# The expert layer moved from the second attention to the first, on one PSUM bank

## What is computed

```
x  = L0_attn_x;  xn = layernorm(x)
# layer 0
a  = attention_0(xn)                    # 16 heads of 64, softmax over queries, W_O
y  = xn + attn(conv(layernorm(xn)))     # 16 heads of 8, causal, rotary, depthwise convolution
h  = layernorm(y)
e  = argmax(h @ router_w)               # one of 4 experts for each position
m  = silu(h @ Wg[e]) * (h @ Wv[e]) @ Wd[e]     # 128 -> 2 x 512 -> 128
x  = x + a + y + m
# layer 1
xn = layernorm(x)
x  = x + flash(xn)                      # 16 heads of 8, causal, two passes over blocks of 64
       + fp4_ffn(xn)                    # 128 -> 352 -> 128, inputs and weights rounded to blocks of FP4
```

## Time and profile before

| | us |
|---|---|
| runs: median (lowest to highest) | 3603.09 (3598.25 to 3603.4) |
| the profiled execution | 3598.52 |
| its span, first to last instruction | 3596.7 |
| TensorE busy (share of the span) | 3086.5 (86%) |
| VectorE busy | 2093.3 (58%) |
| ScalarE busy | 1787.1 (50%) |
| GpSimd busy | 860.3 (24%) |
| mean granted TensorE clock | 0.937 |

### The profile page before, as it was taken

One profiled execution on the slowest core, in us unless ns is written; L12 is line 12 of the kernel. 1 busy time (PEld: TensorE's weight loads), 2 busy tenths in 40 slices (PEclk: granted clock), 3 DMA queues, 4 the chain that ended last, 5 costly groups with the idle time before them and its releaser, 6 DMA issues.

```text
span 3596.7 us, 53224 instructions
## 1 busy us (share of the span) xinstructions
PE 3086.5 (86%) x19535; PEld 1705.8 (47%) x19535; DVE 2093.3 (58%) x4810; ACT 1787.1 (50%) x4252; POOL 860.3 (24%) x1140
## 2 busy tenths in 40 slices
PE   2689898998989899998989889898988989898864
PEld 1245455454545545454545545454554545454432
DVE  5454665756566575657656565665656566554432
ACT  0245555555545455555545555554555555455421
POOL 0000222313222131323123132312213131222323
PEclk7699999999999999999999999999999999999965
DMA  4130303020020302002030301103020110200000
GB/s 104 20 44 1 52 2 47 9 36 20 13 43 2 55 2 44 12 17 40 1 55 2 44 12 22 35 2 55 2 44 12 24 31 7 47 2 14 6 11 3
DMA packets 112901, 89.39 MB, mean 25 GB/s; under 512 B 11203, under 2 KB 107269, under 8 KB 112645
## 3 DMA queue, kind: packets, MB, share of 16 engines
q1 hardware_dynamic: 93956, 70.25, 12.8%
q0 software_dynamic: 4096, 8.40, 0.8%
q10 hardware_dynamic: 14592, 7.34, 0.7%
HBM read 27.05 MB, written 16.19 MB: 12 GB/s over the span
## 4 chain that ended last, share of the span: by engine, by line
PE 59%; DVE 12%; POOL 10%; issue 9%; ACT 5%; DMA 2%; SPq 1%; POOLq 0%; ACTq 0%; DVEq 0%
PE ps L1584 6%; PE ps L1601 6%; PE ps L1819 4%; PE ps L1743 4%; PE ps L1722 4%; PE ps L1656 3%; PE ps L1645 3%; PE ps L1623 3%; DVE nma L1210 3%; PE ps L1632 3%; PE ps L1574 2%; PE ps L1703 2%; PE ps L1884 2%; PE ps L1561 2%; PE ps L1587 2%
## 5 line engine op out<-in xcount | busy, mean ns | idle before, releaser
L877 ACT ACTIVATE share_a<-ps,nma 128x128 f32<-128x128 f32 (+3 forms) x1024 | 530.9, 525 | 443.7 <-DVE nma L1210 442.5
L1210 DVE TENSOR_REDUCE nma<-ps 128x2 f32<-128x256 f32 (+3 forms) x512 | 420.1, 823 | 407.5 <-PE ps L1587 405.4
L945 ACT ACTIVATE share_z<-ps 128x512 f32<-128x512 f32 (+1 forms) x704 | 378.3, 559 | 372.1 <-PE ps L1724 241.7
L1275 DVE TENSOR_REDUCE nmx<-ps 128x1 f32<-128x384 f32 (+3 forms) x704 | 426.1, 635 | 173.9 <-PE ps L1705 162.4
L722 POOL TENSOR_TENSOR vn<-va,rla 128x512 f32<-128x512 f32 x128 | 133.4, 1042 | 1359.1 <-DVE rla L1181 1359.1
L1601 PE MATMUL ps<-share_a,vn 128*64 128x512 f32 (+3 forms) x2048 | 351.4, 492 | 35.7 <-POOL vn L722 34.7
L1703 PE MATMUL ps<-kst,qst 96*128 96x128 bf16 (+3 forms) x1024 | 269.6, 317 | 71.1 <-DMA kst<-part 34.4
L1722 PE MATMUL ps<-qst,kst 99*128 99x512 bf16 (+3 forms) x1024 | 261.6, 304 | 28.2 <-ACT share_z L945 14.9
L798 POOL TENSOR_TENSOR share_s<-share_s 128x352 f32<-128x352 f32 (+1 forms) x80 | 80.1, 1001 | 770.7 <-DVE share_s L1084 770.5
L1601 PEld LDWEIGHTS ps<-share_a,vn 128*64 128x64 f32 x2048 | 150.8, 151 | 227.9 <-issue 154.2
L1584 PE MATMUL ps<-kq_odd 64*128 64x128 f32 (+3 forms) x1024 | 220.5, 508 | 38.7 <-ACT share_a L877 36.9
(11 more groups left out here) (250 smaller groups left out, 5727.0 us busy)
## 6 DMA issues: line engine op xcount, KB each, us to landing
qst<-part SPq DMA_DIRECT2D x144, 128.0 KB
kst<-part SPq DMA_DIRECT2D x144, 128.0 KB
share_r<-h_sorted SPq DMA_DIRECT2D x16, 448.0 KB, 3.5
y_sorted<-share_a ACTq DMA_DIRECT2D x16, 448.0 KB, 3.0
xin<-in_L_attn_x SPq DMA_DIRECT2D x16, 256.0 KB, 3.9
xk<-xn SPq DMA_DIRECT2D x16, 256.0 KB, 17.5
xres<-in_L_attn_x SPq DMA_DIRECT2D x16, 256.0 KB
out<-xn SPq DMA_DIRECT2D x16, 256.0 KB, 17.4
```

Of the source, the lines that this page charges most:

```text
L877: activation(pa[:, h % 4, OFF[t]:OFF[t] + P * (t + 1)], ps[:, b + k, 0:P * (t + 1)], ACT.Exp, bias=nma[:, h, t:t + 1], accum_out=la[:, h, ...
L945: activation(pt[:, n % 2, h % 4:h % 4 + k, 0:wd], src, ACT.Exp, scale=SCALE_B)\
L1210: v.tensor_reduce(nma[:, 2 * p:2 * p + 2, t], ps[:, b:b + 2, 0:P * (t + 1)], AX.X, ALU.max, negate=True).then_inc(amax, 1)
L1275: v.tensor_reduce(nmx[:, h:h + k, t], src, AX.X, ALU.max, negate=True).then_inc(bmax_ready, 1)
```

## The change

The expert layer goes into the first half of the round. Its seven tiles run one after another on bank 5 (`MOE_BANK`): each step waits for the evacuation of the step before it. Bank 6 alone is `row_max`'s (and `project_v`'s and `shift_rows`'s), and bank 7 takes the after stream (`divide`, `join`, `project_y`, `transpose3`, `route`, `rank`) beside layer 1's; `exps` keeps banks 5 and 6. `sort` is in two parts. The expert buffers leave `share_a` and `share_g`, which the first attention uses, and lie in `share_r` and `hpad`, which the second attention and the convolution use in the other half. So the next round's `kq 0` and first `scores` no longer wait for the experts, while the first `exps` and the first `attend` evacuation do. All four orders are written anew. On TensorE `project_v` comes first, `row_max 0` comes earlier, `sort 0` stands behind `scores1 4`, the tiles are spread from there to `z 7`, and `ao` now stands ahead of `exps 0`. On VectorE `round_x` comes before `shift_rows`, `split 1` before the last tiles of layer 1. On GpSimd `scatter` moves from behind `spread_queries1` to between `norm 0` and `norm 1`, `gather` to behind `round_x 3`.

```diff
-GATE_BANK, VALUE_BANK = (2, 3), (0, 1)
+MOE_BANK = 5
...
     pe=[
...
+        ("project_v",), ("kq", 0), ("v", 0), ("divide", 0), ("kq", 1), ("scores", 0, 0), ("divide", 1), ("v",
+        1), ("divide", 2), ("scores", 0, 1), ("divide", 3), ("scores", 0, 2), ("join",), ("scores", 0, 3),
+        ("project_y",), ("kq", 2), ("scores", 1, 0), ("scores", 1, 1), ("scores", 1, 2), ("z", 0),
+        ("transpose3",), ("route",), ("v", 2), ("scores", 1, 3), ("rank",), ("kq", 3), ("scores", 2, 0),
+        ("scores", 2, 1), ("scores", 2, 2), ("z", 1), ("v", 3), ("row_max", 0), ("row_max", 1),
+        ("transpose2",), ("keys1",), ("scores", 2, 3), ("row_max", 2), ("queries1",), ("values1",),
...
+        ("row_max", 10), ("scores1", 3), ("scores1", 4), ("sort", 0), ("scores", 3, 1), ("sort", 1),
+        ("row_max", 11), ("scores1", 5), ("row_max", 12), ("gate", 0), ("scores1", 6), ("row_max", 13),
+        ("value", 0), ("scores1", 7), ("turn", 0), ("down", 0), ("row_max", 14), ("gate", 1), ("scores", 3,
+        2), ("z", 2), ("row_max", 15), ("value", 1), ("row_max", 16), ("v", 4), ("turn", 1), ("row_max", 17),
...
+        3), ("row_max", 41), ("probs_T1", 1, 3), ("value", 6), ("row_max", 42), ("mix1", 1), ("row_max", 43),
+        ("z", 7), ("shift_rows",), ("turn", 6), ("project1",), ("down", 6), ("ao",), ("exps", 0), ("exps", 1),
+        ("transpose_xq",), ("exps", 2), ("exps", 3), ("transpose1",), ("gate1", 0), ("exps", 4), ("attend", 0,
...
     pool=[
-        ("norm", 0), ("norm", 1), ("spread_queries1",), ("scatter",), ("norm", 2), ("shift1", 0), ("shift1",
+        ("norm", 0), ("scatter",), ("norm", 1), ("spread_queries1",), ("norm", 2), ("shift1", 0), ("shift1",
...
-        5), ("norm", 6), ("norm", 7), ("round_x", 3), ("round_h", 0, 3), ("round_h", 1, 3), ("round_h", 2, 3),
-        ("gather",), ("round_h", 3, 3),
+        5), ("norm", 6), ("norm", 7), ("round_x", 3), ("gather",), ("round_h", 0, 3), ("round_h", 1, 3),
+        ("round_h", 2, 3), ("round_h", 3, 3),
...
+        hsT = view(share_r, [C, SORTED * P])
+        ysort = view(share_r, [P, SORTED, C])
+        ymT = view(share_r, [P, 2, CHUNKS, P], 1024)
...
+        sg = (view(share_r, [P, DFF], 2048), hpad[:, 2:T + 2])
+        ym = sg
...
@@ TensorE @@
                 def gate(j):
-                    if j == 1:
-                        pe.wait_ge(ao_added, count(i, DENSE["ao_added"], 1))
-                    elif j:
-                        pe.wait_ge(yT_ready, count(i, DENSE["yT_ready"], j - 1))
...
+                    if j:
+                        pe.wait_ge(y_ready, count(i, DENSE["y_ready"], j))
...
                 def value(j):
...
+                    pe.wait_ge(gate_read, count(i, DENSE["gate_read"], j + 1))
...
                 def row_max(u):
-                    wd, b = P * (t + 1), 5 + u % 2
+                    wd, b = P * (t + 1), 6
...
-                    if u >= 2:
-                        pe.wait_ge(bmax_ready, count(nxt, AHEAD["bmax_ready"], u - 1))
+                    else:
+                        pe.wait_ge(bmax_ready, count(nxt, AHEAD["bmax_ready"], u))
...
                 def exps(u):
                     if u == 0:
                         pe.wait_ge(shift_loaded, count(nxt, AHEAD["shift_loaded"], 48))
+                        if i is not None:
+                            pe.wait_ge(y_ready, count(i, DENSE["y_ready"], SORTED))
...
                 def divide(t):
                     if t == 0:
                         pe.wait_ge(by_ready, count(i, AHEAD["by_ready"], 4))
-                    if t >= 2:
-                        pe.wait_ge(yn_ready, count(i, AHEAD["yn_ready"], t - 1))
+                        if prv is not None and (type(prv[0]) is not int or prv[0] + prv[1]):
+                            pe.wait_ge(out_ready, count(prv, BEHIND["out_ready"], 0))
+                    else:
+                        pe.wait_ge(yn_ready, count(i, AHEAD["yn_ready"], t))
...
@@ first places of the ring, TensorE @@
                     elif prv is not None:
-                        pe.wait_ge(y_ready, count(prv, DENSE["y_ready"], SORTED))
+                        pe.wait_ge(aexp_done, count(prv, DENSE["aexp_done"], 4 * HEADS))
+                        if n:
+                            pe.wait_ge(ao_added, count(prv, DENSE["ao_added"], 1))
```

More of the change, by code:

```diff
@@ L148 @@
[L148 to L152, removed]
@@ L163 @@
[L163 to L167, removed]
@@ L168 @@
[L168 to L172, removed]
@@ new lines @@
+        0), ("row_max", 20), ("value", 2), ("scores", 4, 1), ("row_max", 21), ("scores", 4, 2), ("turn", 2),
+        ("row_max", 22), ("z", 3), ("row_max", 23), ("down", 2), ("v", 5), ("gate", 3), ("scores", 4, 3),
+        ("kq", 6), ("row_max", 24), ("value", 3), ("probs_T1", 0, 0), ("row_max", 25), ("scores", 5, 0),
+        ("turn", 3), ("row_max", 26), ("probs_T1", 0, 1), ("row_max", 27), ("scores", 5, 1), ("row_max", 28),
+        ("down", 3), ("scores", 5, 2), ("row_max", 29), ("probs_T1", 0, 2), ("gate", 4), ("z", 4), ("row_max",
@@ new lines @@
+        30), ("probs_T1", 0, 3), ("value", 4), ("v", 6), ("scores", 5, 3), ("row_max", 31), ("kq", 7),
+        ("turn", 4), ("row_max", 32), ("mix1", 0), ("scores", 6, 0), ("row_max", 33), ("scores", 6, 1),
+        ("down", 4), ("row_max", 34), ("scores", 6, 2), ("probs_T1", 1, 0), ("z", 5), ("row_max", 35),
+        ("gate", 5), ("v", 7), ("scores", 6, 3), ("probs_T1", 1, 1), ("row_max", 36), ("value", 5), ("scores",
+        7, 0), ("row_max", 37), ("turn", 5), ("probs_T1", 1, 2), ("row_max", 38), ("scores", 7, 1),
@@ new lines @@
+        ("scores", 5, 1), ("norm", 4), ("row_max", 28), ("scores", 5, 2), ("row_max", 29), ("gate", 4),
+        ("row_max", 30), ("value", 4), ("scores", 5, 3), ("row_max", 31), ("row_max", 32), ("scores", 6, 0),
+        ("row_max", 33), ("mix1", 0), ("scores", 6, 1), ("norm", 5), ("row_max", 34), ("scores", 6, 2),
+        ("gate", 5), ("row_max", 35), ("scores", 6, 3), ("row_max", 36), ("value", 5), ("scores", 7, 0),
+        ("row_max", 37), ("row_max", 38), ("scores", 7, 1), ("norm", 6), ("row_max", 39), ("scores", 7, 2),
@@ new lines @@
+        ("row_max", 40), ("gate", 6), ("scores", 7, 3), ("row_max", 41), ("value", 6), ("norm", 7),
+        ("row_max", 42), ("mix1", 1), ("project1",), ("row_max", 43), ("round_x", 0), ("round_x", 1),
+        ("round_x", 2), ("shift_rows",), ("ln0_stats",), ("ln0_root",), ("ln0_apply",), ("ln1_apply",),
+        ("conv",), ("up1", 0), ("round_h", 0, 0), ("project", 0, 0), ("round_h", 0, 1), ("project", 0, 1),
+        ("round_h", 0, 2), ("add_ao",), ("up1", 1), ("round_h", 1, 0), ("round_h", 1, 1), ("round_h", 1, 2),
@@ new lines @@
+        ("project_v",), ("scores", 0, 2), ("scores", 0, 3), ("kq", 2), ("scores", 1, 0), ("scores", 1, 1),
[3 rows of a table added]
+        ("scores1", 3), ("scores1", 4), ("sort", 0), ("scores", 3, 1), ("sort", 1), ("scores1", 5), ("gate",
+        0), ("scores1", 6), ("scores1", 7), ("turn", 0), ("down", 0), ("gate", 1), ("scores", 3, 2), ("z", 2),
+        ("shift1", 0), ("shift1", 1), ("v", 4), ("turn", 1), ("shift1", 2), ("scores", 3, 3), ("down", 1),
+        ("shift1", 3), ("kq", 5), ("gate", 2), ("scores", 4, 0), ("scores", 4, 1), ("scores", 4, 2), ("turn",
```

246 lines of the change are left out of this document (107 added, 139 removed), and 10 rows, old and new, of the table act.

## The result

The changed kernel takes 3749.55 us (median; 3745.26 to 3751.01), the one before 3602.35: ratio 1.0409, 95% interval 1.0391 to 1.0427. I had said 3570 and 3500 to 3655. The profiled execution spans 3743.4 us against 3596.7, so 146.7 us are to be found.

What follows compares the result with a forecast made beforehand. TensorE was taken as the bound, with 35.2 us of waits in a 205.1 us round. 3598.5 - 45 (14 rounds at -3.2) + 31 (prologue) - 5 (first round) - 13 (last) = 3566, said as 3570; range 3500 to 3655.

Steps and rivals of the forecast that it cites:

- The prologue: Before the rounds, with nothing between the `row_max`: 44 units take 64 us on one bank instead of 33.4, +31.
- The first round: Poorer round after the prologue: gains some 5 us, expert steps filling a first attention without the second block.
- rival A: One-bank waits eat the gain: at 0.15 us more per return, +6.6 a round, 3659 us; chance 0.34.
- First part: Round start to `row_max 0`: 29.7 us of work, waits 11.8 against 9.3; `row_max 0` at +41.5, before +43.8.
- 2.5 lost: Up to `row_max 0`: extra waiting, as `scatter` ahead of `norm 1` on POOL delays `z 1` to 37.4.
- A clock that falls: Looser second half of the round: listed last among possible omissions that would prove the forecast wrong, without a size.
- Middle: `row_max 0` to `z 7`: 91.2 us of work, 22 of it new; one-bank `row_max` shortfalls 3.4; `z 7` at +145.4.
- Second part: From `z 7` to the round's end: 49.5 us of work, waits 7 against 10.1 before.
- The first `exps` waited 1.75 us for the shift rows' copy, which now lies under `ao`: Behind `z 7`: one of three waits said to go, 1.75 us, covered by `ao`.
- The last round: Poorer final round: experts done earlier shorten its 58.5 us tail to some 43, first attention grows 3: -13 us.

Runs made afterwards that it cites:

- `after_z1_filled`: Changed kernel with three useless 128x512 matmuls ahead of `z 1`, in its wait for GpSimd: 3698.2 us, ratio 1.0274.
- `after_no_register_loads`: The spaced kernel with constants instead of TensorE's seven register loads of expert numbers behind `sort 0` and `sort 1`: 3604.9 us, ratio 1.002.
- the spaced kernel: Changed kernel with scatter back behind `spread_queries1`, the prologue's `row_max` on two banks, and `row_max` 0 to 10 spaced on TensorE: 3628.3 us, ratio 1.0079.
- `after_ao_behind_exps`: The spaced kernel with `exps 0` and `exps 1` ahead of `ao`, as in the kernel before: 3719.5 us, ratio 1.0332.

## Why the prediction was wrong

**The prologue** was right: forecast 64 us for the 44 units and `kq 0` at 219, measured 64.3 and 219.4.

**Where the error lies.** Twelve full rounds from seam to seam, before from 574.4 and after from 637.7, cut as in the prediction (means, us; the seam is `kq 0` before and `project_v` after, the first step of the round):

| | before | after | change | forecast |
|---|---|---|---|---|
| seam to `row_max 0` | 45.4 | 44.7 | -0.7 | -2.3 |
| `row_max 0` to `z 7` | 82.5 | 109.0 | +26.4 | +22.3 |
| `z 7` to the next seam | 80.0 | 60.8 | -19.2 | -23.2 |
| round | 207.9 | 214.5 | +6.6 | -3.2 |

That is 9.8 us a round, 137 in 14 rounds, of the 179 between the forecast 3566 and the profiled 3745. The first round adds 25, the last 13. The time also lies beyond 3659, rival A's price and the dearest that I had named. So no single term failed; these did, in order of the round.

**First part: `z 1`'s wait was priced at full clock.** I wrote that `z 1` waits about 3 us for GpSimd, "2.5 lost". The wait was right: in the rounds with 3 us of low time `z 1` starts at +37.5 (I had 37.4), and where nothing lowers the clock ahead of `row_max 0` that comes at +41.5 (`after_z1_filled`), my own number. What I had put at nothing is the lower clock behind such a wait. `z 1` takes 3.5 to 4.5 us instead of 2.4 in every full round, and the term of 2.5 measured 5.7 us a round when the scatter was put back, 87 us in all, six tenths of the loss. My prices were all at full clock, from a round with 3 us of low time that I took for typical; the average round of before loses 1.6 us more in this part too, so that the net error here is 1.6 and not 3.2. "A clock that falls" stood at the very end of the prediction, for the second half and without a price.

**Middle: seven register loads were priced at nothing.** I took `sort` for its transposes alone, 0.8 us. Without the loads this part is 106.1 us instead of 108.2 (`after_no_register_loads` against the spaced kernel), 2.1 of the 4.1 missing. The other 2 are open. They are not rival A's returns on one bank: `row_max` waits 2.9 us for VectorE where I had 3.4. Only the side of before was off, 1.1 where its trace has 2.1.

**Second part.** 56.5, measured 59.4 in the best round and 60.8 on average, with hardly any low time. "The first `exps` waited 1.75 us for the shift rows' copy, which now lies under `ao`": the copy does lie under it, and `after_ao_behind_exps` shows what it costs if not. That the 1.75 stood in 3 of 14 rounds only does not explain the miss, for in the others `z 7` was as much slower (80.0 us in the average round and 79.7 in the one that I studied). No run took this part alone, and why it is 3 to 4 us longer than forecast stays open.

**The first round.** "-5", measured +19.6. I had the tiles fill this first attention. The stretch from `row_max 0` to `shift_rows` took 68.2 us before; in the new order without tiles it takes 78.6 on two banks and 87.7 on one, and 105.7 with the tiles. So 10.4 are the order, 9.1 the bank, and 18.0 the tiles, for 22.2 of work: they hardly fill anything there. Low time rises along with it (10, 16, 21 and 23 us) and is in these numbers. Behind it only about 19 come back (69.7 to 50.8).

**The last round.** "-13", measured -1.4 between the last two `take_over` and +1.0 behind. I did not try why, and the cause stays open.

Taken together in ratios: scatter 2.4, prologue 0.3 to 0.9, neighbours 0.6: from 1.0409 to 1.0079. What is left of the difference with the loads moved in both kernels is 0.9976 against 0.9925, half a per cent, 15 us by the medians. In the profiled executions the twelve rounds are as long (206.2 and 206.0) and the stretch from the first to the second `take_over` is 9 us longer (219.4 and 210.3). So the first round is most of what is seen there; no run tried it.

## What to carry to other kernels

Price a wait of TensorE with the clock behind it: look at several rounds and their granted clock before taking one as the measure, compare rounds with equal low time, and test a wait by filling it with useless matmuls. When a step moves, count what its engine executes without a row of its own, register loads above all, and don't credit a wait to the releaser that the row names before looking at the same place in other rounds. One bank for a chain cost little here where other work stood between its steps (`row_max` waited 2.9 us a round for VectorE and 2.1 on two banks), and 30.5 us a round where it did not. Measure it with that work in place: the pair without the tiles gave a price that the full kernel doesn't show.

## What the runs showed of the hardware

- Useless matmuls made the kernel 51 us faster: 2.6 us of work in a wait of 3.4 us, low time 12.8 to 5.7 us a round.
- Identical rounds of one execution differ by up to 8.5 us (210.7 and 219.2), in step with the time at the lower clock (3 and 24 us).
- One bank for 44 units cost 504 us in an order with 18 pairs of neighbours, and 109 us in one with 4 pairs (without the expert layer).
